# Two attention blocks, two expert blocks, on one core: where the polynomial stage's weights are split and its first tile is started, and how the output is copied

## The reference, cut to what matters

```python
x = x + _L0_xattn_ref(...)          # cross-attention to ctx
x = x + _L0_attn_ref(...)           # attention
x = x + _L0_ffn_ref(...)            # low-rank experts
x = x + _L1_xattn_ref(_layernorm(x), ctx_768, Wq, bq, Wk, bk, Wv, bv, Wo, bo)
x = x + _L1_attn_ref(_layernorm(x), Wq1, Wk1, Wq2, Wk2, Wv, Wout)
x = x + _L1_ffn_ref(_layernorm(x), router_w, wg, wu, wd)      # 8 experts, best 2 of each row
```

## Time and profile before

| | |
|---|---|
| median of 3 runs | 1782.2 us (1782.05 to 1783.52) |
| time of the profiled execution | 1781.48 us |
| its span in the trace | 1779.8 us |
| busy: PE, PEld | 1563.6 us (88%), 1122.0 us (63%) |
| busy: DVE, ACT, POOL | 1251.2 us (70%), 987.4 us (55%), 677.9 us (38%) |
| mean granted TensorE clock | 0.944 of full |

### The profile page before, as it was taken

One profiled execution on the slowest core, in us unless ns is written; L12 is line 12 of the kernel. 1 busy time (PEld: TensorE's weight loads), 2 busy tenths in 40 slices (PEclk: granted clock), 3 DMA queues, 4 the chain that ended last, 5 costly groups with the idle time before them and its releaser, 6 DMA issues. The chain is left out here.

```text
span 1779.8 us, 43534 instructions
## 1 busy us (share of the span) xinstructions
PE 1563.6 (88%) x16191; PEld 1122.0 (63%) x16191; DVE 1251.2 (70%) x2854; ACT 987.4 (55%) x2210; POOL 677.9 (38%) x796
## 2 busy tenths in 40 slices
PE   6968999999957886799999999499993599999996
PEld 3535777777645665577777776245552477877874
DVE  7858999999746777588888887577775754454431
ACT  5547888888633443466666666333332555565541
POOL 4557777777511110211221121145552233333332
PEclk9979999999969998899999999699996799999998
DMA  6111111111140000001110113401001675575422
GB/s 228 45 59 36 29 46 46 46 47 46 35 172 1 2 1 1 28 27 36 36 36 27 36 36 138 163 1 37 14 13 64 208 224 149 153 201 159 122 37 68
DMA packets 50104, 126.93 MB, mean 71 GB/s; under 512 B 6913, under 2 KB 19553, under 8 KB 49889
## 3 DMA queue, kind: packets, MB, share of 16 engines
q1 hardware_dynamic: 44914, 112.64, 19.5%
q0 software_dynamic: 5008, 11.80, 3.4%
HBM read 110.83 MB, written 15.68 MB: 71 GB/s over the span
## 5 line engine op out<-in xcount | busy, mean ns | idle before, releaser
L106 PE MATMUL e_pGU<-XT,WB 128*128 128x128 f16 x1344 | 231.0, 221 | 16.1 <-issue 10.9
L107 PE MATMUL e_pGU<-XT,WB 128*128 128x128 f16 x1344 | 230.8, 221 | 0.0
L108 PE MATMUL e_pGU<-XT,WB 128*128 128x128 f16 x1344 | 230.7, 221 | 0.0
L2665 DVE SCALAR_TENSOR_TENSOR WB<-raw,WB 128x1024 f16<-128x1024 f32 x96 | 116.3, 1231 | 79.7 <-ACT WB L2814 79.7
L106 PEld LDWEIGHTS e_pGU<-XT,WB 128*128 128x128 f16 x1344 | 133.1, 99 | 21.5 <-issue 19.1
L107 PEld LDWEIGHTS e_pGU<-XT,WB 128*128 128x128 f16 x1344 | 133.1, 99 | 2.0 <-issue 0.4
L108 PEld LDWEIGHTS e_pGU<-XT,WB 128*128 128x128 f16 x1344 | 133.1, 99 | 0.0
L1782 POOL TENSOR_TENSOR XT<-dzo,XT 128x128 f32 (+1 forms) x32 | 13.7, 427 | 283.9 <-ACT XT L1922 283.9
L2648 POOL TENSOR_TENSOR XT<-e_mf,XT 128x256 f16<-128x256 f32 x84 | 59.0, 702 | 162.2 <-ACT XT L2828 162.2
L715 POOL TENSOR_TENSOR crn<-css,mhalf 128x8 f32<-128x8 f32 x64 | 108.6, 1697 | 5.3
L2814 ACT ACTIVATE WB<-raw 128x1024 f16<-128x1024 f32 x96 | 97.9, 1044 | 14.7 <-PE e_pY L108 13.7
(11 more groups left out here) (581 smaller groups left out, 5765.4 us busy)
## 6 DMA issues: line engine op xcount, KB each, us to landing
raw<-in_WE SPq DMA_DIRECT2D x96, 512.0 KB, 4.7
raw<-in_W SPq DMA_DIRECT2D x37, 512.0 KB, 7.7
ctxin<-in_ctx SPq DMA_DIRECT2D x32, 384.0 KB, 3.4
ctxin<-in_ctxT SPq DMA_DIRECT2D x32, 384.0 KB
cv<-vlat SPq DMA_DIRECT2D x32, 96.0 KB
X<-in_x SPq DMA_DIRECT2D x8, 256.0 KB, 8.5
vlat<-vl SPq DMA_DIRECT2D x8, 256.0 KB, 2.0
dv<-vrem SPq DMA_DIRECT2D x128, 0.8 KB
```

Of the source, the lines that this page charges most:

```text
L106: pe.matmul(out, lh, rh, start=first, stop=False, skip_group_check=shared)
L107: pe.matmul(out, lh, rl, start=False, stop=False, skip_group_check=shared)
L108: return pe.matmul(out, ll, rh, start=False, stop=last, skip_group_check=shared)
L2665: dve.scalar_tensor_tensor(WB[w][:, 1, a], ring[n][:, :], WS, WB[w][:, 0, a], ALU.mult, ALU.subtract)\
```

## The change

1. **Weights.** The 15 pieces of `poly`'s weights are loaded one at a time during `cross1` (SP, `following`). ACT splits the high part of one piece in every even body from b = 2 (`next_high`), DVE the low part in every odd body from b = 3 (`next_low`), between `probs_low` and `value_low`. The splits in `poly` go, with the waits on them. `W5` is allocated for both stages.
2. **Loops.** `walk` writes all 32 bodies of `cross1` out. There is no hardware loop any more.
3. **First tile.** At the end of `cross1`, PE makes the first output product (12 matmuls) between the last scores and the last transposes. POOL adds the bias row to tile 0. DVE makes the residual and the statistics before the last `out_sum`. POOL makes the power ahead of the last `out_low`, and ACT the normed rows ahead of the last `out_high`. In `poly`, PE starts with the transpose of them.
4. **`poly`'s transfers.** SP issues 11 loads of the first expert's weights at once behind the small ones. The twelfth waits for the first transpose. DVE waits for `p_in` before anything else.
5. **Table.** 26 columns in place of 34. `past`, `values` and the numbers compared for `lane` are f16, with one more small copy on DVE (`numbers16`) before the plan.
6. **End.** SP copies `sums` to the output as soon as all scatters but the last have landed. The last scatter goes to the output itself, with a bounds check in place of the spare rows, and waits for the copy.

```diff
@@ perceiver
+            c45 = ctx.enter_context(ExitStack())
+            st["W5"] = c45.enter_context(nc.sbuf_tensor("W5", [P, 2, sum(st["W5cols"])], F16, side="right"))
+            st["firstrow"], st["firstya"] = raw[:, 2 * STAGE:2 * STAGE + D], raw[:, 3 * STAGE:3 * STAGE + D]
@@ walk
-    body(0, 0, False, True)
-    with eng.Fori(0, (B - 2) // 2) as i:
-        body(i * 2 + 1, 1, True, True)
-        body(i * 2 + 2, 0, True, True)
-    body(B - 1, 1, True, False)
+    for b in range(B):
+        body(b, b % 2, b > 0, b + 1 < B)
@@ cross1, SP
+            for b in range(2, B + 1):
+                if b < B:
+                    context(b, b % 2, True)
+                if b > 2:
+                    tail(b - 1, (b - 1) % 2, True)
+                if b - 2 < len(cols5):
+                    following(b - 2)
+            sp.wait_ge(sig["d_w5lo"], 4)
+            sp.dma_start(firstrow, d["rows"][2:3, :].broadcast_to([P, D])).then_inc(sig["d_row"], 16)
@@ cross1, POOL
+            def after():
+                pool.wait_ge(sig["d_row"], 16)
+                pool.tensor_tensor(X[:, 0, :], X[:, 0, :], firstrow, ALU.add).then_inc(sig["d_xb"], 1)
+                pool.wait_ge(sig["d_fst"], 3)
+                pool.tensor_tensor(rs[:, :], mv[:, 2:3], st["mhalf"][:, 0:1], ALU.pow).then_inc(sig["d_fpow"], 1)
+                pool.wait_ge(sig["d_fpow"], 1)
+                pool.tensor_scalar(rsm[:, :], rs[:, :], mv[:, 0:1], -1.0, ALU.mult, ALU.mult).then_inc(sig["d_fpow"], 1)
+                out_low(B - 1)
@@ cross1, DVE
+            def first_residual():
+                dve.wait_ge(sig["d_xb"], 1)
+                dve.wait_ge(sig["d_first"], 1)
+                dve.scalar_tensor_tensor(X[:, 0, :], pK[0][:, :], 1.0 / WS, X[:, 0, :], ALU.mult, ALU.add).then_inc(sig["d_xf"], 1)
...
+                dve.bn_stats(stt[:, :], X[:, 0, :]).then_inc(sig["d_fst"], 1)
...
+                dve.bn_aggr(mv[:, 0:2], stt[:, :]).then_inc(sig["d_fst"], 1)
...
+                dve.tensor_scalar(mv[:, 2:3], mv[:, 1:2], EPS, None, ALU.add).then_inc(sig["d_fst"], 1)
+            def next_low(n):
+                a = slice(at5[n], at5[n] + cols5[n])
+                dve.wait_ge(sig["d_w5hi"], n + 1)
+                dve.scalar_tensor_tensor(W5[:, 1, a], raw5[n], WS, W5[:, 0, a], ALU.mult, ALU.subtract).then_inc(sig["d_w5lo"], 1)
@@ body
                     probs_low(b - 1, 0)
                     probs_low(b - 1, 1)
+                if b % 2 and b >= 3:
+                    next_low((b - 3) // 2)
                 value_low(2 * b + 1, u, 1)
@@ after
                     probs_low(B - 1, half)
+                first_residual()
                 out_sum(B - 1)
@@ cross1, ACT: body, after
                 value_high(2 * b + 1, u, 1)
+                if b % 2 == 0 and b >= 2:
+                    next_high((b - 2) // 2)
...
                 probs_high(B - 1, 1)
+                act.wait_ge(sig["d_fpow"], 2)
+                act.activation(firstya, X[:, 0, :], ACT.Identity, bias=rsm[:, 0:1], scale=rs[:, 0:1]).then_inc(sig["d_fy"], 1)
                 out_high(B - 1)
@@ cross1, PE: after
                 scores(B - 1, (B - 1) % 2)
+                pe.wait_ge(sig["d_w5lo"], 2)
+                pe.wait_ge(sig["d_olo"], BPT + STARTS["d_olo"])
+                for k in range(CK):
+                    i = product(pe, pK[0][:, :], hl(XT, k, slice(0, P)), hl(Wo1, k), k == 0, k == CK - 1)
+                i.then_inc(sig["d_first"], 1)
                 turn_probs(B - 1)
@@ poly, SP
-            for n in range(2, 12):
-                sp.wait_ge(sig["p_wlo"], n + 1)
+            for n in (0, 1, 2, *range(4, 12)):
                 ahead(n)
+            sp.wait_ge(sig["p_ta_T"], 1)
+            ahead(3)
@@ poly, DVE
-            for n in range(*OP):
-                split(n)
+            sig.begin(dve, "p_xo", "p_a_st", "p_a_mv", "p_a_var")
+            dve.wait_ge(sig["p_in"], 32)
...
-                if s == 0:
-                    for n in range(*MP):
-                        split(n)
...
-                if s == 1:
-                    for n in range(*UP):
-                        split(n)
@@ experts, SP
+            sp.wait_ge(sig["e_plan"], 1)
+            total = number(sp, 2 * E1, MOST)
+            sp.wait_ge(sig["e_put"], (total + 1) * 16)
+            sp.dma_start(st["out"], sums[0:TOK, :]).then_inc(sig["e_out"], 16)
             sp.wait_ge(sig["e_end"], 1)
-            sp.dma_start(st["out"], sums[0:TOK, :]).then_inc(sig["e_out"], 16)
-            sp.wait_ge(sig["e_out"], 16)
@@ experts, POOL
+            pool.wait_ge(sig["e_out"], 16)
             pool.wait_ge(sig["e_y"], total + 1)
             sig.passed(pool, "pool")
-            scatter()
-            pool.wait_ge(sig["e_put"], (total + 2) * 16)
+            pool.indirect_dma_start(st["out"], bass.IndirectOffsetOnAxis(ap=torow[:, 0:1], axis=0), yo[:, :], None, compute_op=ALU.add,
+                                    bounds_check=TOK - 1, oob_is_err=False).then_inc(sig["e_last"], 16)
+            pool.wait_ge(sig["e_last"], 16)
@@ experts, DVE
+            dve.tensor_copy(numbers16[:, :], slots[:, 0:T]).then_inc(sig["e_values"], 1)
...
-            dve.tensor_tensor(past[:, :, :], spot[:, :].unsqueeze(2).broadcast_to([P, PAIRS, TABLE + 1]),
-                              bounds[:, :].unsqueeze(1).broadcast_to([P, PAIRS, TABLE + 1]), ALU.is_ge).then_inc(sig["e_spot"], 1)
+            dve.tensor_tensor(past[:, :, :], spot[:, :].unsqueeze(2).broadcast_to([P, PAIRS, USED + 1]),
+                              bounds[:, 0:USED + 1].unsqueeze(1).broadcast_to([P, PAIRS, USED + 1]), ALU.is_ge).then_inc(sig["e_spot"], 1)
```

More of the change, by code:

```diff
@@ L1725, in cross1 @@
         hl = lambda t, *ix: (t[(slice(None), 0, *ix)], t[(slice(None), 1, *ix)])
+        W5, cols5 = st["W5"], st["W5cols"]
+        at5 = [sum(cols5[:n]) for n in range(len(cols5))]
+        X, firstrow, firstya = st["X"], st["firstrow"], st["firstya"]
+        (stt, mv, rs), (_, _, rsm) = st["work"]
+        Wo1 = W5[:, :, 0:CK * D].rearrange("p a (k n) -> p a k n", k=CK)
+        raw5 = [*st["W5in"][0:12], *st["W5in"][0:2], st["W5in"][12]]
         @block.sync
@@ L1744, in _, with following @@
             tail(1, 1, False)
[L1745 to L1758, removed]
+            def following(n):
+                if n in (12, 13):
+                    sp.wait_ge(sig["d_w5lo"], n - 11)
+                sp.dma_start(raw5[n], d["W"][:, WAT["o1"] + at5[n]:WAT["o1"] + at5[n] + cols5[n]]).then_inc(kept[f"w5_in{n}"], 16)
+            for b in range(2, B + 1):
[7 more added lines that the diff above has]
+            sp.dma_start(firstrow, d["rows"][2:3, :].broadcast_to([P, D])).then_inc(sig["d_row"], 16)
         @block.gpsimd
@@ L1789, in body @@
                     out_low(b - 1)
-            walk(pool, body, None, lambda: out_low(B - 1))
+            def after():
[6 more added lines that the diff above has]
+                out_low(B - 1)
+            walk(pool, body, None, after)
         @block.vector
@@ L2156, in _ @@
                 if t is not None:
-                    power("a", t)
+                    if t:
+                        power("a", t)
                     if t + 1 < NT:
@@ L2183, in _ @@
         def _(dve):
-            def split(n):
-                a = slice(at[n], at[n] + widths[n])
-                dve.wait_ge(sig["p_whi"], n + 1)
-                dve.scalar_tensor_tensor(W[:, 1, a], pieces[n][:, 0:widths[n]], WS, W[:, 0, a], ALU.mult, ALU.subtract).then_inc(sig["p_wlo"], 1)
             def stats(n, t, ready):
@@ L2315, in _ @@
         def _(act):
-            def split(n):
-                act.wait_ge(kept[f"w5_in{n}"], 16)
-                act.activation(W[:, 0, at[n]:at[n] + widths[n]], pieces[n][:, 0:widths[n]], ACT.Copy, scale=WS).then_inc(sig["p_whi"], 1)
             def scale(n, t, y):
@@ L2357, in rows_high @@
                 act.activation(xr[t % 2][:, 0, :], ye[:, :], ACT.Copy).then_inc(sig["p_xrhi"], 1)
-            for n in range(*OP):
-                split(n)
+            sig.begin(act, "p_a_y")
             for s in range(SLOTS):
@@ L2372, in _ @@
                     mat_high(0, b)
-                if s == 0:
-                    split(MP[0])
-                    split(MP[0] + 1)
-                if t is not None:
+                if t:
                     scale("a", t, ya)
-                if s == 0:
-                    for n in range(MP[0] + 2, MP[1]):
-                        split(n)
                 if r is not None:
@@ L2541, in experts @@
     TABLE = MOST + SLOTS + 2
+    USED = MOST + 2
     SPARE = TOK
@@ L2735, in _ @@
                 half = slice(i * NT, (i + 1) * NT)
-                dve.tensor_tensor(lane[:, half, :], slots[:, 0:T].unsqueeze(1).broadcast_to([P, NT, T]),
-                                  within[:, half].unsqueeze(2).broadcast_to([P, NT, T]), ALU.is_equal).then_inc(sig["e_lane"], 1)
+                dve.tensor_tensor(lane[:, half, :], numbers16[:, :].unsqueeze(1).broadcast_to([P, NT, T]),
```

(1 more changed line is left out.)

78 lines of the change are left out of this document (35 added, 43 removed).

## The result

| | before | after |
|---|---|---|
| median | 1782.9 us (1782.1 to 1784.6, 4 runs) | 1766.8 us (1764.4 to 1767.9, 4 runs) |
| profiled execution, its span | 1781.5, 1779.8 | 1767.6, 1765.8 |

The ratio of the times is 0.9907, with a 95% interval of 0.989 to 0.9924: 16.1 us faster, where 23.8 were forecast, so 7.7 us are missing. 1766.8 lies outside the range of 1753 to 1764.

The account below looks back on a forecast made before the run. PE was taken as the bound, busy 88% of the span, idle at the seam, the plan of `experts` and the end. -20.1 + 0.9 + 0 - 4.6 = -23.8 us gave 1758.4 us, range 1753 to 1764.

Parts of the forecast that it names:

- The unrolled loop: `cross1` bodies written out: removes register work PE already hides, adds instruction fetch; cost 0, with `cross0` as straight-code evidence.
- The half clock at the start of `poly`: How long PE stays at the lower clock from the first projection on: 0 taken, 1.6 us as bound.
- The seam: From `cross1` to `poly`'s first projection: 20.1 us won in `poly`, 0.9 us lost at `cross1`'s end.
- The rival step of some 6 us for a function's first call: POOL's power step at the seam: library load costs about 6 us more, 1764.4 in all; counted with the worse seam.
- The end: Output copy just hidden before the last scatter, POOL's DRAIN of 3.75 us stays and ends the kernel: 4.6 us won.
- the rival without it: Kernel's end: DRAIN goes with the copy, so the end gives 8.4 us, 1754.6 in all; chance 0.2.
- Splits, loads, table: Splits and loads in `cross1` bodies hidden in existing waits, smaller table hidden behind PE's register loads: 0 each.
- The rival on fetch: Unrolled `cross1`: PE stalls 2 us in each of 30 bodies, 60 us lost, 1818; chance 0.03 beyond 24 us.
- The seam gives less: Seam: dear POOL queue, late `p_in`, longer half clock, 6.5 us less, 1764.9; chance 0.13 for 2 to 6.5 worse.

Follow-up runs that it names:

- Run 2: Kernel before with only the 32 bodies of `cross1` written out: ratio 1.0025 to the kernel before.
- run 5: Changed kernel plus five unread 16-column matmuls on PE after `cross1`'s last outputs, moving later code by 10 instructions: ratio 0.9904 to the kernel before.
- run 6: Kernel before with `cross1`'s bodies written out, plus five small matmuls moving PE's later code by 10 instructions: ratio 1.0012 to the kernel before.
- run 10: Changed kernel with DVE's `p_in` wait later, POOL's tile-0 bias in body 24, SP awaiting the last scatter, sixty small PE matmuls: ratio 0.9878 to before.
- Run 4: Changed kernel with unread 128x512 matmuls filling PE's waits at the seam and at the turn of slots in `poly`: ratio 0.9899 to the kernel before.
- run 3: Changed kernel without its new end (part 6): ratio 0.9914 to the kernel before.
- run 8: Changed kernel where SP, not POOL, waits for the last scatter's landing: ratio 0.989 to the kernel before.
- run 11: Changed kernel as it is, timed again: ratio 0.9903 to the kernel before.
- Run 1: Kernel before with only the change's new end (part 6): ratio 0.9977 to the kernel before.
- run 12: Changed kernel with later `p_in` wait, bias in body 24, SP awaiting last scatter, five small matmuls, 12 `poly` filler matmuls: ratio 0.9842 to before.

## Why the prediction was wrong

**The unrolled loop is the step that failed.** Its "Cost 0" priced the fetch inside `cross1`, and there it was right: 60.00 of 60 us. It didn't ask what written-out bodies do to all PE code behind them. They move it, and in `experts` PE stands still behind taken branches, in every kernel here, 2.5 to 3.3 us at the tile looked at. What depends on the place is whether it stands still again some instructions further on (0.4 to 4.4 us), and whether both together bring the clock down. Run 2 measured the written-out bodies alone: 5.9 us in `experts`, and by the ratio 2.7 to 6.1 us, so some 4.4 of the 7.7 us that are missing, if they cost the changed kernel as much (its `experts` is 4.5 us longer). Runs 5, 6 and 10 moved the stalls by moving code. The Trainium skill (Runtime: NRT & Kernel Launch, "Instruction fetch mechanics") says that code comes in blocks of 16 KiB, 256 instructions, whose crossing is mostly hidden, and that a taken branch stalls when its target isn't in the window at hand. The runs agree that taken branches stall, and show a second stall soon behind some of them. That each such stall is the crossing of a block was argued from the counts, not seen.

**The half clock at the start of `poly`** was taken at 0 with 1.6 us as bound. In the profile of after it cost 4.0 us: 1.2 in the first projections, then a second fall at 1150 us, behind waits of 1.67 and 1.50 us that before has too. Run 4 shows that it is the clock, runs 3, 8 and 11 that the same PE program escapes it in other executions. The bound left out that a second fall can follow in the next slot. How much of the missing 7.7 us of the medians is the half clock's stays open: it stands in two of the eight profiles with the new seam and no fillers (after and run 5), no run counted how often it comes, and the changed kernel had nearly the same ratio both times it was run (0.9907 and 0.9903), though only the first profile shows it.

**The seam** came out at 19.4 us for 19.2, but partly by luck, since errors cancel. POOL's power step was warm (1.4 us less than taken). Against that `dnm` cost 0.7 us beside POOL's bias, the change of stages 0.35 us (from `out_low`'s start to that of `poly` 1.96 us, before 1.61), and the first projection came 0.2 us later behind the start of `poly`. The rival step of some 6 us for a function's first call did not show: the power step took 0.56 + 0.27 us, and ACT's rows start at its end.

**The end** gave 4.0 for 4.6: the copy took 1.9 us longer than the one read off in the earlier trace rows and came 0.5 us late. The forecast had it "just hidden". That `DRAIN` stays was right, so the rival without it falls. Run 1, where the copy took 8.4 us, gained 4.8.

**Splits, loads, table:** hidden as forecast (*plan* +0.2 us). `p_in` ended last at the seam, and no load got in front of it. The rival on fetch counted about 135 matmuls in a body; the trace has 103 (2,060 in 20 bodies). Nothing in the sum hung on it.

**The rivals.** *The seam gives less* would have landed near the measured time for a wrong reason. *Instruction fetch* was looked for in the wrong stage, and with a price per body. The prediction named the stall of taken branches beside it, and the profile of before already had PE's waits of 1.9 and 2.9 us put down to issue in `experts`.

## What to carry to other kernels

Code on an engine that branches isn't free to move: where a stage's waits are put down to issue behind branches, price every edit ahead of it that changes the number of instructions, and try a few paddings before judging an edit of 0.3%. Read the profile's waits without a semaphore in the stages that the change doesn't touch. Where a change moves PE's short waits at a stage's start, put the cost of half clock there into the range (here up to 4 us), since it comes in some executions and not in others.

## What the runs showed of the hardware

- A stall behind a taken branch can have a second one 3 to 92 instructions later: 3.31 + 2.41 us in after, 6.00 in run 2. 10, 34, 72 and 120 added instructions moved it by as many, or removed it. Most are shorter the further behind they stand: 2.41 to 4.38 us at 6, 1.2 to 2.1 at 42 to 55, 0.89 at 92; the one of 0.44 us at 21 in run 12 breaks the row.
- An operation of 128x4 on DVE took 0.88 us in place of 0.17 while POOL added 128x512.
- POOL's last `DRAIN` took 3.75 us behind a landed scatter, and 6.53 when it began with the scatter's start (run 8).
- A copy of 2 MB from HBM to HBM took 8.3 or 8.4 us alone (before, runs 2 and 3), and 8.4 to 10.9 us beside the last tile.
- A matmul filler that runs at half clock (14 matmuls in 5.07 us, run 4) can hold a barrier: the seam got 3.4 us longer there.
